# Moving row maxima, scale diagonals, scale products and a layer normalisation between VectorE, ScalarE and GpSimd in the last stage of a two-layer decoder

## The reference

```python
def act_quant(x):
    scale = 127.0 / jnp.clip(jnp.max(jnp.abs(x), axis=-1, keepdims=True), 1e-05)
    return jnp.clip(jnp.round(x * scale), -128, 127) / scale
...
h = bit_linear(x, w1)                                # act_quant(x) times ternary w1
h = depthwise_conv1d(h.transpose(0, 2, 1), conv_w, conv_b)
h = jax.nn.silu(h.transpose(0, 2, 1))
return bit_linear(h, w2)                             # act_quant(h) times ternary w2
...
x = _layernorm(x + _L1_ffn_ref(x, ...), axis=-1)     # the program's output
```

## Time and profile before

| | us |
|---|---|
| median of three runs (2534.89 to 2537.69) | 2537.33 |
| the profiled execution, its own time | 2531.09 |
| its span | 2529.3 |
| PE busy | 2314.0 (91%) |
| DVE busy | 1548.7 (61%) |
| ACT busy | 1230.1 (49%) |
| POOL busy | 671.0 (27%) |

### The profile page before, as it was taken

The page is one execution under the profiler, slowest core; times in us unless marked ns, Lnnn a source line. Parts: engine busy times, 40 slices in busy tenths (PEclk is TensorE's granted clock), DMA queues, the critical chain, the costliest instruction groups (busy, mean ns, idle before and its releaser), DMA issues.

```text
span 2529.3 us, 38996 instructions
## 1 busy us (share of the span) xinstructions
PE 2314.0 (91%) x13952; PEld 1308.4 (52%) x13952; DVE 1548.7 (61%) x3113; ACT 1230.1 (49%) x2842; POOL 671.0 (27%) x973
## 2 busy tenths in 40 slices
PE   8889999989988999998998999999899899999776
PEld 3665544545465544554556554454555655445343
DVE  4665652469866553347977646245797755515688
ACT  5762312259675322127967431223886833122395
POOL 0003140027401223013820213202480031310366
PEclk9999999999999999999999999999999999999988
DMA  8001011010210110101030111001003010000000
GB/s 310 18 11 51 24 47 34 1 50 1 90 52 10 51 50 22 34 12 39 9 132 2 33 51 31 19 33 50 1 12 130 2 60 24 31 17 1 0 1 34
DMA packets 58996, 99.87 MB, mean 39 GB/s; under 512 B 13237, under 2 KB 13749, under 8 KB 58297
## 3 DMA queue, kind: packets, MB, share of 16 engines
q1 hardware_dynamic: 58808, 97.39, 11.7%
HBM read 88.99 MB, written 8.39 MB: 39 GB/s over the span
## 4 chain that ended last, share of the span: by engine, by line
PE 64%; ACT 17%; DVE 14%; issue 4%; POOL 0%; DMA 0%; ACTq 0%; POOLq 0%; DVEq 0%; SPq 0%
PE psum L418 23%; PE psum L412 14%; ACT prob L836 7%; PE psum L444 4%; PE psum L504 3%; DVE neg_max L1123 3%; ACT f_z L1023 2%; PE psum L472 2%; ACT f_a L1021 2%; DVE bn L1071 2%; PE psum L817 2%; PE psum L570 2%; DVE f_a L1130 1%; DVE f_top L1412 1%; PE psum L590 1%
## 5 line engine op out<-in xcount | busy, mean ns | idle before, releaser
L418 PE MATMUL psum<-weights,mixed 128*128 128x512 f32 x768 | 341.7, 595 | 0.0
L412 PE MATMUL psum<-xT,weights 128*128 128x512 f32 x768 | 338.7, 595 | 2.4 <-ACT xT L872 2.4
L836 ACT ACTIVATE prob<-psum,neg_max 128x128 f32<-128x128 f32 (+3 forms) x512 | 264.5, 543 | 110.0 <-DVE neg_max L1123 110.0
L1450 POOL TENSOR_SCALAR var<-stats 128x1 f32<-128x1 f32 x192 | 64.1, 334 | 949.9 <-DVE stats L1072 949.9
L1123 DVE TENSOR_REDUCE neg_max<-psum 128x1 f32<-128x128 f32 (+3 forms) x512 | 217.1, 481 | 80.8 <-PE psum L509 46.1
L872 ACT COPY xT<-psum 128x512 f32<-128x512 f32 x128 | 70.9, 587 | 363.6 <-PE psum L472 363.6
L1463 POOL TENSOR_TENSOR f_a<-f_a,f_z 128x256 f32<-128x256 f32 x256 | 204.9, 811 | 114.2 <-DVE f_a L1130 111.3
L418 PE MATMUL psum<-weights,xT 128*128 128x512 f32 x512 | 232.3, 598 | 0.0
L412 PEld LDWEIGHTS psum<-xT,weights 128*128 128x128 f32 x768 | 142.9, 190 | 172.3 <-issue 170.8
L418 PEld LDWEIGHTS psum<-weights,mixed 128*128 128x128 f32 x768 | 141.7, 190 | 170.6 <-issue 169.8
L1102 DVE TENSOR_TENSOR x<-psum,x 128x512 f32<-128x512 f32 x128 | 88.3, 690 | 230.7 <-PE psum L418 177.8
(11 more groups left out here) (240 smaller groups left out, 4073.1 us busy)
## 6 DMA issues: line engine op xcount, KB each, us to landing
xT<-in_xT SPq DMA_DIRECT2D x8, 1024.0 KB, 6.3
x<-in_x SPq DMA_DIRECT2D x8, 1024.0 KB, 8.8
out<-x SPq DMA_DIRECT2D x16, 512.0 KB, 2.8
weights<-in_a_k SPq DMA_DIRECT2D x4, 1024.0 KB, 5.4
weights<-in_a_q SPq DMA_DIRECT2D x4, 1024.0 KB, 5.2
weights<-in_a_v SPq DMA_DIRECT2D x4, 1024.0 KB, 5.2
w1f<-in_w SPq DMA_DIRECT2D x4, 1024.0 KB, 15.1
w2f<-in_w SPq DMA_DIRECT2D x4, 1024.0 KB, 17.4
```

The costliest lines, as they stand in the source:

```text
L412: last = mm(bank[:, 0:n], weights[weight][:, c, heads(g)], rhs(c), start=(c == 0), stop=(c == C - 1))
L418: last = mm(bank, lhsT(c), weights[weight][:, c, :], start=(c == 0), stop=(stop and c == C - 1))
L836: last = run(sb["prob"][:, slot, o:o + keys], bank[:, o:o + keys], ACT.Exp, bias=sb["neg_max"][:, n, qc, j:j + 1], accum_out=sb["a_sum"][: ...
```

## The change

Four edits, all in stage F:

1. At the rounding, DVE takes the maxima in four instructions of one tile each, and each waits only for its own tile's normalisation.
2. The four diagonals of a rounding are made by POOL in place of ACT.
3. Of the products by the scale, DVE does four (0 to 3 of sub-tile 3) in place of eleven; POOL does 28 in place of 21.
4. `f_norm` goes from DVE to ACT; POOL makes `shift` for it as a third small instruction behind each `f_out`.

```diff
 def scaled_by_dve(s, i):
-    return s == NSUB - 1 or (s == NSUB - 2 and i >= 5)
+    return s == NSUB - 1 and i < M // 4
...
@@ ScalarE
-                elif kind == "e_norm":
-                    t, = arg
-                    act.wait_ge(q["e_shift_ready"], at("e_shift_ready", t + 1))
+                elif kind in ("e_norm", "f_norm"):
+                    stage, t = (STAGE_E, arg[0]) if kind == "e_norm" else (STAGE_F, 2 * arg[0] + arg[1])
+                    act.wait_ge(q["e_shift_ready"], at("e_shift_ready", T * (stage - STAGE_E) + t + 1))
                     run(x[:, t, :], x[:, t, :], ACT.Identity, scale=sb["rstd"][:, t:t + 1], bias=sb["shift"][:, t:t + 1])\
-                        .then_inc(counter("x_normed", STAGE_E)[0], 1)
+                        .then_inc(counter("x_normed", stage)[0], 1)
                 elif kind == "f_round":
                     w, = arg
-                    act.wait_ge(q["f_unit_ready"], at("f_unit_ready", w + 1))
-                    for t in range(WT):
-                        run(sb["f_diag"][:, w, t, :], ident[:], ACT.Copy, scale=sb["f_ax"][:, w, t:t + 1]).then_inc(q["f_diag_ready"], 1)
@@ VectorE, f_round
-                    normed(dve, STAGE_E, WT * (w + 1))
-                    link(v.tensor_reduce(am, x[:, WT * w:WT * w + WT, :], AX.X, ALU.max, apply_absolute_value=True))
+                    for t in range(WT):
+                        normed(dve, STAGE_E, WT * w + t + 1)
+                        top = v.tensor_reduce(am[:, t:t + 1], x[:, WT * w + t, :], AX.X, ALU.max, apply_absolute_value=True)
+                    link(top)
@@ VectorE
-                elif kind == "f_norm":
-                    normalise(STAGE_F, 2 * arg[0] + arg[1])
@@ GpSimd, rstd
-                    if stage == STAGE_E:
+                    if stage in (STAGE_E, STAGE_F):
                         pool.wait_ge(ready, 2 * n + 2)
                         g_.tensor_scalar(sb["shift"][:, t:t + 1], sb["stats"][:, t, 0:1], sb["rstd"][:, t:t + 1], -1.0, ALU.mult, ALU.mult)\
                             .then_inc(q["e_shift_ready"], 1)
@@ GpSimd
+                if kind == "f_round":
+                    w, = arg
+                    pool.wait_ge(q["f_unit_ready"], at("f_unit_ready", w + 1))
+                    for t in range(WT):
+                        g_.tensor_scalar(sb["f_diag"][:, w, t, :], ident[:], sb["f_ax"][:, w, t:t + 1], None, ALU.mult)\
+                            .then_inc(q["f_diag_ready"], 1)
```

More of the change, by code:

```diff
@@ L55 @@
        "d_logits_ready": 1, "d_e_ready": 1, "d_shares_ready": 1, "d_mixed": 8, "d_v_weighed": 6, "e_pad": 1, "e_exp_ready": 2,
-       "f_pad": 4, "e_shift_ready": 8, "f_tmp_ready": 8, "f_xq_ready": 8, "f_diag_ready": 16, "f_unit_ready": 2, "f_tap_done": 128, "f_tap2_done": 64, "f_conv_done": 64,
-       "f_silu_done": 32, "f_scaled": 21, "f_scaled_dve": 11, "f_hq_ready": 16, "f_out_filled": 8, "f_out_taken": 8,
+       "f_pad": 4, "e_shift_ready": 16, "f_tmp_ready": 8, "f_xq_ready": 8, "f_diag_ready": 16, "f_unit_ready": 2, "f_tap_done": 128, "f_tap2_done": 64, "f_conv_done": 64,
+       "f_silu_done": 32, "f_scaled": 28, "f_scaled_dve": 4, "f_hq_ready": 16, "f_out_filled": 8, "f_out_taken": 8,
        "bias_added": 24, "ctx_loaded": 48,
```

## The result

| | before | after |
|---|---|---|
| median of four runs each (us) | 2536.11 (2530.85 to 2537.69) | 2548.66 (2547.61 to 2551.0) |
| profiled execution, its own time | 2531.09 | 2549.03 |
| its span | 2529.3 | 2547.2 |

A forecast was written before the change was run, and what follows sets the result against it. PE is busy 91% of the span, but stage F is bound by a chain alternating between DVE, ACT and PE. Terms 12.2 + 0.5 + 2.4 + 2.4 - 2.8 - 2.7 = +12.0 on 2531.09, plus 6.2 to the median: 2549; range 2537 to 2560.

The forecast's parts named there:

- Products 4 to 7 of sub-tile 3: In the finish, POOL's products start behind the statistics and run slower than DVE's: +3.05 us per batch row, +12.2 over four.
- The end: At the kernel's very end, the last normalisation on ACT takes longer and the shift adds about 0.3: +0.5 us.
- The clock: Rival: PE's clock falls in the longer gap before its last sixteen matmuls, +2.5 us per batch row, 2559; chance 0.17.
- The finish: the rest: In the finish, sub-tile 2's three products and two normalisations leave DVE, yet `f_out(2, 0)` starts unchanged: 0, between -0.4 and +0.5.
- the lock: Rival: at the roundings, DVE's `f_tmp` and POOL's diagonals block one another, 0.7 us or more at each of eight, 2555; chance 0.08.
- Hidden blocks 48 to 56: Two normalisations added to ACT fill its wait and push by 0.7; taken as +0.6 us each, +2.4 for four.
- The next batch row: At its first transposes, PE waits 0.8 us for ACT's copy behind two normalisations; three times, +2.4.
- The roundings: Both roundings get shorter through tile-by-tile maxima and diagonals on POOL: -2.8 us for the first, -2.7 for the second.
- The first rounding: The first hidden block starts 0.5 to 0.85 us earlier, since ACT can copy while PE transposes; four times 0.7, -2.8.
- The second: Second rounding: `f_xq` can start earlier, net -0.4 us each in batch rows 0 to 2, -1.5 in row 3, together -2.7.
- The normalisation: The last normalisation on ACT costs 0.5 us at the end, 2.4 in the next batch rows, 2.4 in the hidden blocks.

The follow-up runs named there:

- e_fill: The changed kernel with ten unused matmuls added on PE while it waits for `f_quant` of POOL's products; median 2548.25 us, ratio 1.0058 against the kernel before.
- e_sub3_pool: The kernel before with only products 4 to 7 of sub-tile 3 moved to POOL; median 2547.17 us, ratio 1.0050 against before.
- e_round: The kernel before with only the roundings changed: maxima tile by tile, diagonals on POOL; median 2526.39 us, ratio 0.9967 against before.
- e_norm_back: The changed kernel with the last normalisation on DVE again, the other three edits kept; median 2541.80 us, ratio 1.0034 against the kernel before.
- e_norm: The kernel before with only the last normalisation moved to ACT; median 2550.45 us, ratio 1.0058 against before.

## Why the prediction was right, and where it was not

The direction, the time (2549 forecast, 2548.66 measured) and the leading term stand. But that the number agrees so closely is luck: two errors cancel. On the profiled pair the sum was +12.0 and the trace shows +17.9; and the 6.2 us from the profiled execution to the median, which hold for before, do not hold for after, where the profiled execution lies 0.37 above its median. Term by term:

- **Products 4 to 7 of sub-tile 3**, forecast +12.2 (3.05 per batch row): right in mechanism and size; with the clock held (e_fill) stretch IV shows +12.6. Products start 1.26 behind the statistics (forecast 1.32), and stretch IV grows by 4.19 in batch row 1, of which 0.95 is the clock and 3.24 the wait. The split of PE's matmuls into two groups is seen only where the clock doesn't fall (e_sub3_pool, row 2). The end, forecast +0.5, is stretch V, +0.43.
- **The clock** was a rival with 0.17, priced at +2.5 per batch row. The wait is the one forecast (2.89 for 3.0), and the clock did fall; the price is 0.95, because the mean clock was 0.70 and not the 0.54 of the earlier trace rows, and because PE would have waited 0.54 between its two groups anyway. So forecast and rival were no alternatives: the rival happened at about two fifths of its price, +3.6 in all.
- **The finish: the rest**, forecast 0 between -0.4 and +0.5: wrong, +5.5. The step reckoned POOL's products, ACT and PE of sub-tile 2 one by one, and left the scale of sub-tile 3, which DVE makes at the same moment, at its old length. That scale is the term it had at nothing: its tensor_scalars take 4.57 for 1.06. The two shifts that the step did count are what brings 0.84 of the 1.50 per row, by the moment at which POOL starts. I cited the lock for `f_tmp` and the new diagonals, where both kinds of instruction are large, and did not look for small tensor_scalar instructions beside POOL's new work. Where the lock was looked for it costs DVE 0.06 us; where it was not, 3.5 us of stretched instructions in each batch row.
- **Hidden blocks 48 to 56**, forecast +2.4, 0.6 each: stretch II shows 0.2 in rows 0 to 2, so the term was a third of its forecast there. The sum of +1.8 comes near only by the 1.22 of row 3, where e_round has 0.6 without this edit. In e_norm_back rows 0 to 2 show 0.0: the 0.2 is the normalisation's.
- **The next batch row**, forecast +0.8 each: PE's wait is 0.45, and up to L768 the changed kernel takes 0.6 to 0.7 more than e_norm_back in each of rows 1 to 3.
- **The roundings**, forecast -2.8 and -2.7: from L768 to `f_out(0, 0)` the changed kernel shows -8.4. The first rounding gives 0.45, 0.8, 0.9 and 0.9 (forecast 0.7), so it was right in size. The second gives 0.6 in rows 0 to 2 (forecast 0.4) and 3.5 in row 3 (forecast 1.5). Of this last one a part that was not measured by itself is the clock's: e_round, with the same roundings and more time at 1.2 GHz, gains 1.4 there. e_round's two readings, -8.4 by the ratio and -4.8 by the spans, lie on both sides of the forecast -5.5.
- **The normalisation** was priced at +5.3 in all (0.5 at the end, 2.4 in the next batch rows, 2.4 in the hidden blocks), and costs 4.6 to 7.5 in the changed kernel, but not at the places that were priced: 2.8 of the 7.5 are in stretch III. That it costs 14.7 alone was not seen, and not needed: the products cover it.

Single edits against before sum up to -8.4 + 14.7 + 3.0 + 12.7 = +22.0, and the change costs 13.2. The 8.8 between them are mostly the normalisation's cover (its 10.7 in stretch IV, less the 2.8 that it adds to stretch III); without it the sum is 7.3, and e_norm_back has 8.6. By the spans the sum is +29.4 for +17.9, and without the normalisation +14.5 for +10.4, so the edits add up only to within some 4 us.

## What to carry to other kernels

Before work is moved to GpSimd, list what VectorE does in the same microseconds, the smallest instructions first: a tensor_scalar on two numbers per partition can wait a whole GpSimd instruction, and a chain of four of them did, four times in a row. Cut a change of several edits into single ones even when it loses as a whole: the two rounding edits alone make the kernel 8.4 us faster (ratio 0.9967, 95% interval 0.9954 to 0.9979), and this was hidden behind a loss of some 20. In an engine's queue in program order, work that nobody waits for belongs behind work that somebody waits for, and the price of the wrong order depends on what else is late (here 14.7 us or 5 to 7). That the other order gives the price back was not tried.

## What was not expected of the hardware

- **Small tensor_scalar instructions wait for GpSimd as long as large ones.** 128x2 on DVE: 0.17 to 0.23 us alone, 0.92 to 1.19 in the lines above when a POOL tensor_tensor of 1.23 us was running; the reduction and the reciprocal between them kept 0.17. The Trainium skill, "SBUF — State Buffer", section "Who interferes with whom", gives the rule (a tensor_scalar can take the shared ports, a reduction can't, and the other engine blocks for the whole instruction), and the trace agrees.
- **Two tensor_tensor instructions with both inputs in SBUF also hinder one another** (5.71 for 2.50, 6.79 for 4.93), which the same section says of DVE with two SBUF inputs. But `f_tmp` on DVE beside POOL's tensor_scalar took 1.73 for 1.67: there POOL's instructions gave way, not DVE's. In the first rounding POOL's four take 1.26, 0.77, 0.60 and 0.60, and the last two run behind the end of `f_tmp`. What decides who gives way was not tried.
- **The same gap lowers PE's clock one time and not another.** In e_norm_back stretch IV takes 11.80, 12.77, 11.80 and 12.72. In batch row 0 PE waits 2.92 us and the window behind the wait has clock 1.00; in batch row 1 it waits 2.92 too:

```profile
675.30:680.00 4.70, 4.07 (x26) 1.74 (x29) 1.05 (x2) 2.67 (x4) 1.30 (x2) 1.00 0.01 3
...
1292.00:1298.60 6.60, 4.72 (x14) 1.76 (x15) 0.23 (x1) 3.78 (x4) 3.09 (x3) 0.74 0.22 81
```

The step between the two is again some 0.95 us. In e_norm the same happens with a wait of 2.36 us: the clock falls in rows 0 and 3 and not in 1 and 2. What tips it is open.
